# Attention block with routed experts: the positions added by GpSimd before the transposes, the transposed x taken out of PSUM by ScalarE

## The chip, the cores and the metric

The kernel runs on one core of a Trainium2 chip. The metric is the device time of one execution in microseconds (us), the median of several. A core has five engines with instruction streams of their own: TensorE (PE: matmuls and transposes into PSUM), VectorE (DVE), ScalarE (ACT), GpSimd (POOL) and SyncE (SP, which here only issues DMAs). They meet through semaphores. SBUF is the large on-chip memory, PSUM the small one that PE writes.

## The reference

128 sequences of 64 tokens, 128 features each. Cross-attention with 16 heads of 8, then a mixture of 8 experts of which each token takes 2. All of it in float32:

```
n  = layernorm(x)
pe = position encodings, 64 x 128
q  = (n + pe) @ Wq.T + bq          k = (ctx + pe) @ Wk.T + bk        v = ctx @ Wv.T + bv
s  = q.k * 8**-0.5 - 1e7 * (padding mask or causal mask)
x  = x + softmax(s).v @ Wo.T + bo
g  = softmax(gelu(layernorm(x) @ wg1 + bg1) @ wg2), the two largest kept
x  = x + sum over the two experts of g_e * gelu(layernorm(x) @ w_in[e]) @ w_out[e]
```

The change is about the term `n + pe` in the first of these products.

## The kernel before, in words

The 8192 tokens are 64 tiles of 128 rows (two sequences each). A **stage** s is U = 4 tiles; there are NS = 16 stages. The attention part runs the `body(s, i, par)` of each engine for s = 0 to 15, and in each body the four tiles u = 0 to 3. The tile counter is t = 4s + u. No scheduler is at work: every engine's stream is written out by hand, with waits on counters, and what stands where in a body is the order in which it runs.

Per tile, in `body`: PE transposes the probabilities of tile t (L407), makes the scores of tile t+2 into the one score buffer S2 (L391, L397, after `s_sub` says that DVE has emptied it), multiplies with the values (L420, L425) and projects (L434). DVE takes the row maxima of tile t+1 (L814), subtracts them into `sm` (L818), and then divides tile t-1 (L826, L828) and adds the residual of tile t-2 (L836). ACT copies the transposed probabilities out of PSUM (L710) and takes the exponentials of tile t+1 (L652).

Per stage, and one to three stages ahead or behind:

- `ln1_stats` and `ln1_variance` on DVE (L791, L796), `rstd_1` on POOL (L1159 to L1164), `ln1_norm` on ACT (L666), which writes the normalised x, `xn`, of stage s+2 at u = 2.
- `t_x(s+1)` on PE at u = 0 (L362) transposes `xn` into the PSUM bank W0. `x_evac(s+1)` on DVE (L801), still at u = 0, adds the transposed positions `pe_s` and writes `xT`. `project_q(s+1)` on PE at u = 1 (L371) reads it, `q_evac` on ACT (L635) brings q to SBUF.
- `add_positions(s+3)` on POOL at u = 3 (L1150) adds `pe_s` to the context for the keys; `project_k` (L367) and `k_evac` (L631) follow, and SP then spreads the keys to a block layout `kx` with 16 small DMAs (`spread_keys`, L263).
- `make_mask(s+1)` on DVE at u = 0 (L808) reads two SBUF tiles, `mask_in` and `causal`.
- The routing of stage s-2 runs through all engines: ACT `xt2_evac` (L694), `gate_gelu` (L700) and `gate_exp` (L704), PE `gate_hidden` (L464) and `gate_logits` (L470), DVE `take_logits`, `gate_probs`, `find_two_largest` (L876, L878: a small copy from SBUF to SBUF) and `select` (L883, L888). POOL forms the pairs (L1207) and scatters the rows of stage s-3 to HBM with indirect DMAs (L1222). This starts with s = 2; the counting of stage s-3 (L895 to L909 on DVE, the rank matmuls on PE) with s = 3.

Before the first body each engine has a short prologue. ACT issues two lists of constant loads (L657 and L660). The semaphore `s_w` counts the first list, 6 loads, the last of them `bq`; PE, POOL, ACT and DVE wait for all of it. On POOL the prologue is `add_positions(0)`, `rstd_1(0)`, then a memset that clears the second half of `kx` (L1179), then `add_positions(1)`, `rstd_1(1)`. SP waits in L275 for both halves of `kx` to be cleared, and issues `spread_keys(0)` after that; what follows in SP's queue is one long list of issues, up to the keys of stage 2:

```
sp.wait_ge(s_kev, 1)
sp.wait_ge(s_kz, 2)
spread_keys(0)
```

After the attention part the rows are read back in 91 blocks by pair of experts (L583 to L603 on PE, L753 and L770 on ACT, L1103 to L1129 on DVE, L1259 on POOL). The change has nothing in it.

Of the kernel before, what the change touches and what calls it, by code (L numbers as in the profile page):

```python
# [12 lines left out]
ALU = mybir.AluOpType  # L13
# [3 lines left out]
P = 128  # L17
# [56 lines left out]
def build(nc, x, ctxT, mask, wqT, bq, wkT, bk, wvT, bv, woT, bo, wg1, bg1, wg2, w_in, w_out, out):  # L74

    pe_c = nc.inline_tensor(np.ascontiguousarray(position_encodings().T), name="pe_t")
    ident_c = nc.inline_tensor(np.eye(P, dtype=np.float32), name="ident")
# [36 lines left out]
    with ExitStack() as ctx:  # L114
# [35 lines left out]
        xn = sb("xn", [P, U, D])  # L150
        minus_half, eps_s = sb("minus_half", [P, U]), sb("eps_s", [P, U])
# [49 lines left out]
        s_wg2z = sem("wg2_zeroed")  # L201
        s_w2, s_w3 = sem("attention_constants_in"), sem("routing_constants_in")
        NW, NW2, NW3 = 6, 7, 5 + 2 * U
# [39 lines left out]
        with nc.Block() as block:  # L243
# [113 lines left out]
            def _(pe):  # L357
                def t_x(s):

                    pe.wait_ge(s_xn, s + 1)  # L360
                    for u in range(U):
                        last = nc.tensor.transpose(W0[:, u * P:(u + 1) * P], xn[:, u, :], ident[:, :])  # L362
                    last.then_inc(s_xt, 1)
# [264 lines left out]
            def _(act):  # L628
# [8 lines left out]

                def v_evac(s):
                    act.wait_ge(s_v, s + 1)
                    if runs(s, 2):  # L640
                        act.wait_ge(s_pv, (s - 1) * U)
                    src = W0[:, :].rearrange("r (g j p c) -> r g j p c", j=2, p=2, c=DH)
                    for b in range(2):
                        for p in range(2):
                            o = b * VB + p * DH
                            last = nc.scalar.activation(vx[p * 64:p * 64 + 64, s % 2, :, :, o:o + DH],
                                                        src[b * 64:b * 64 + 64, :, :, p, :], ACT.Copy)
                    last.then_inc(s_vev, 1)
# [5 lines left out]
                for dst, src in ((pe_s[:, :], pe_c.ap()), (wk_s[:, :], wkT), (ident[:, :], ident_c.ap()), (wq_s[:, :], wqT),  # L654
                                 (bk_s[:, :], bk.rearrange("(p a) -> p a", a=1)),
                                 (bq_s[:, :], bq.rearrange("(p a) -> p a", a=1))):
                    act.dma_start(dst, src).then_inc(s_w, 16)  # L657
# [22 lines left out]
                k_evac(0, 0)  # L680
                act.wait_ge(s_bqs, 1)
                q_evac(0, 0)
                act.wait_ge(s_xt, 1)
# [22 lines left out]
                def body(s, i, par):  # L706
                    for u in range(U):
# [4 lines left out]
                        if u < U - 1 or runs(s, 0, NS - 2):  # L712
                            exps(t + 1, u + 1)
                        if u == 0 and runs(s, 2):
                            xt2_evac(s - 2)
# [71 lines left out]
            def _(dve):  # L787
# [10 lines left out]

                def x_evac(s):
                    dve.wait_ge(s_xt, s + 1)  # L800
                    nc.vector.tensor_tensor(xT[:, :].rearrange("p (b k) -> p b k", k=L),  # L801
                                            W0[:, :].rearrange("p (b k) -> p b k", k=L),
                                            pe_s[:, :].unsqueeze(1).broadcast_to([P, 2 * U, L]), ALU.add
                                            ).then_inc(s_xTs, 1)
# [181 lines left out]
                x_evac(0)  # L986
# [15 lines left out]
                def body(s, i, par):  # L1002
                    for u in range(U):
# [41 lines left out]
                        if u == 0 and runs(s, 0, NS - 2):  # L1045
                            x_evac(s + 1)
# [98 lines left out]
            def _(pool):  # L1145
# [7 lines left out]

                def rstd_1(s):
# [23 lines left out]
                rstd_1(0)  # L1178
                nc.gpsimd.memset(kx[:, 1, :, :], 0.0).then_inc(s_kz, 1)  # L1179
                pool.wait_ge(s_w2, 16 * NW2)  # L1180
                add_positions(1)
                rstd_1(1)
                pool.wait_ge(s_cvec, 1)
# [42 lines left out]
                def body(s, i, par):  # L1226
                    for u in range(U):
# [16 lines left out]
                        if u == 3 and runs(s, 0, NS - 4):  # L1244
# [4 lines left out]
                            add_positions(s + 3)  # L1249
                        if u == 3 and runs(s, 3, NS - 2):  # L1250
# [58 lines left out]
```

## Time and profile before

| | |
|---|---|
| median of 3 runs | 618.54 us (616.45 to 619.35) |
| the profiled execution, its own time | 617.17 us |
| its span, first to last instruction | 615.4 us |
| DVE busy | 473.8 us, 77% of the span; 96.8% in a stage of the attention part |
| PE busy | 504.6 us, 82% |
| ACT busy | 391.3 us, 64% |
| POOL busy | 272.0 us, 44% |
| attention part | to about 389 us |
| expert part | from there to the end |

In the timelines each line gives the start in us, the busy time in us of the instruction (or of a run of equal ones), engine, line, operation, tiles and shapes, and in brackets the idle time of the engine before it with what ended it. Instructions of one engine are pipelined, so the next can start a little before the one ahead has ended: what an instruction costs its engine is the distance to the next start. SPq, ACTq and POOLq are the DMA-issuing parts of these engines.

### The profile page before, as it was taken

What the parts mean: (1) busy time and instruction counts of PE and PEld (TensorE: products, weight loads), DVE (VectorE), ACT (ScalarE), POOL (GpSimd) and SP (SyncE); (2) the same over time, 40 slices, a digit from 0 to 9 for tenths busy, and PEclk for the clock granted to TensorE, in tenths of its full rate; (3) what the DMA queues carried; (4) which work ended last, traced back from release to release, by engine and by line L of the source; (5) the groups of instructions that cost most, each with busy time, mean ns of one, the idle gap of its engine ahead of it and who ended that gap; (6) DMA issues with size and microseconds to landing.
All of it is one profiled execution on the core that took longest, in us unless ns stands there. A gap on an engine that the chain in (4) does not pass through costs nothing.

```text
span 615.4 us, 19115 instructions
## 1 busy us (share of the span) xinstructions
PE 504.6 (82%) x6643; PEld 383.1 (62%) x6643; DVE 473.8 (77%) x1587; ACT 391.3 (64%) x723; POOL 272.0 (44%) x451
## 2 busy tenths in 40 slices
PE   2489899988988888888998885477577999999992
PEld 0145555645655555554654554377567999999992
DVE  3598899999999999999999997355644666666661
ACT  2156687878878877877787873356333666666660
POOL 4131333463473364365345333345522555555552
PEclk9999999999999999999999997678977999999997
DMA  4137212212212312222111001422555333443300
GB/s 111 17 77 226 62 48 63 75 54 59 79 55 56 84 51 65 71 55 73 32 46 46 20 29 37 125 59 66 170 163 149 103 106 107 108 108 90 80 21 1
DMA packets 41806, 46.86 MB, mean 76 GB/s; under 512 B 9738, under 2 KB 33555, under 8 KB 41248
## 3 DMA queue, kind: packets, MB, share of 16 engines
q1 hardware_dynamic: 34144, 32.28, 20.3%
q0 software_dynamic: 5984, 12.90, 6.2%
q8 instruction: 55, 0.90, 0.6%
q10 hardware_dynamic: 1584, 0.46, 0.3%
q14 instruction: 39, 0.32, 0.2%
HBM read 28.52 MB, written 18.58 MB: 77 GB/s over the span
## 4 chain that ended last, share of the span: by engine, by line
DVE 35%; PE 31%; issue 16%; SPq 12%; DMA 2%; POOL 1%; ACT 1%; ACTq 1%; POOLq 0%; DVEq 0%
PE probs_t L592 13%; PE bank L603 13%; DVE smax L814 10%; DVE rden L826 8%; SPq L263 5%; SPq L322 3%; DVE rows L836 2%; PE scores L583 2%; DVE stat L842 2%; DVE stat L791 1%; DVE negmask L808 1%; DVE left L883 1%; SPq L315 1%; DMA bq_s<-bq 1%; DVE mv L847 1%
## 5 line engine op out<-in xcount | busy, mean ns | idle before, releaser
L1259 POOL DMA_INDIRECT out<-yb,token_row x91 | 89.1, 979 | 108.2 <-DVE token_row L1118 84.7
L592 PE MATMUL probs_t<-xbT,wi 128*128 128x128 f32 x728 | 102.7, 287 | 10.8 <-ACT wi L770 8.3
L753 ACT ACTIVATE hb<-probs_t 128x512 f32<-128x512 f32 x91 | 54.4, 598 | 86.0 <-PE probs_t L592 86.0
L710 ACT ACTIVATE pt<-probs_t 128x1024 f32<-128x1024 f32 x64 | 65.6, 1025 | 66.0 <-PE probs_t L407 65.6
L592 PEld LDWEIGHTS probs_t<-xbT,wi 128*128 128x128 f32 x728 | 94.2, 202 | 12.5 <-ACT wi L770 9.2
L603 PE MATMUL bank<-wo,hb 128*128 x728 | 100.8, 284 | 0.1
L603 PEld LDWEIGHTS bank<-wo,hb 128*128 128x128 f32 x728 | 92.5, 199 | 0.7 <-issue 0.5
L391 PE MATMUL scores<-kx,qT 64*64 64x512 f32 x512 | 70.6, 621 | 27.2 <-DVE sm L818 15.1
L814 DVE TENSOR_REDUCE smax<-scores 128x16 f32<-128x1024 f32 x64 | 77.8, 1216 | 12.1 <-PE scores L397 11.0
L1222 POOL DMA_INDIRECT routed_rows<-rows,pos x64 | 64.2, 1004 | 37.5 <-DVE pos L909 19.5
L818 DVE TENSOR_TENSOR sm<-scores,smax 128x1024 f32<-128x1024 f32 x64 | 78.3, 1224 | 2.2
L1125 DVE SCALAR_TENSOR_TENSOR part<-bank,gate,xb 128x128 f32<-128x128 f32 x91 | 31.9, 350 | 62.0 <-PE bank L603 62.0
L407 PE MATMUL probs_t<-ident_s,sm 128*128 128x128 f32 x512 | 67.7, 276 | 0.9 <-ACT sm L652 0.9
L652 ACT ACTIVATE sm<-sm 128x1024 f32<-128x1024 f32 x64 | 67.3, 1051 | 0.2
L420 PEld LDWEIGHTS bank<-pt,vx 128*32 128x32 f32 x2048 | 31.9, 110 | 54.7 <-DVE onT L828 46.3
L420 PE MATMUL bank<-pt,vx 128*32 128x64 f32 x2048 | 42.3, 223 | 27.5 <-DVE onT L828 26.4
L770 ACT COPY wi<-wi_all 128x256 f32 x182 | 63.7, 402 | 1.2 <-DVE expert_oh L959 1.2
L826 DVE RECIPROCAL rden<-bank 128x128 f32<-128x128 f32 x64 | 60.0, 937 | 2.9 <-PE bank L425 2.9
L407 PEld LDWEIGHTS probs_t<-ident_s,sm 128*128 128x128 f32 x512 | 57.9, 142 | 4.6 <-issue 4.6
L1159 POOL TENSOR_TENSOR var<-mv,eps_s 128x4 f32<-128x4 f32 x16 | 3.2, 201 | 121.4 <-DVE mv L796 116.6
L391 PEld LDWEIGHTS scores<-kx,qT 64*64 64x64 f32 x512 | 13.8, 132 | 59.5 <-DVE sm L818 33.6
L1103 DVE COPY xbT<-scores 128x128 f32<-128x128 f32 x91 | 26.1, 287 | 26.4 <-PE scores L583 26.2
(119 smaller groups left out, 885.9 us busy)
## 6 DMA issues: line engine op xcount, KB each, us to landing
xb<-routed_rows SPq DMA_DIRECT2D x91, 132.5 KB, 2.2
ctx_in<-ctx_t SPq DMA_DIRECT2D x16, 256.0 KB, 3.1
x_in<-x SPq DMA_DIRECT2D x16, 256.0 KB, 3.8
kx<-kT SPq DMA_DIRECT2D x256, 16.0 KB
routed_rows<-padding_rows SPq DMA_DIRECT2D x29, 132.5 KB
out<-yb,token_row POOLq DMA_INDIRECT x91, 2.3
mask_in<-mask SPq DMA_DIRECT2D x16, 64.0 KB, 4.2
wi_all<-w_in SPq DMA_DIRECT2D x1, 1024.0 KB, 9.8
```

Of the source, the lines that this page charges most:

```text
L391: nc.tensor.matmul(S_bank[half][b * L:(b + 1) * L, :].rearrange("p (h k) -> p h k", k=L), qT[r, par, o:o + L], kx[r, par, :, o:o + L], sta ...
L407: last = nc.tensor.transpose(PT_bank[j // 4][:, (j % 4) * P:(j % 4 + 1) * P], pr[:, j * P:(j + 1) * P], ident[:, :])
L420: nc.tensor.matmul(XB[g * VB:(g + 1) * VB, b * L:(b + 1) * L], v[:, c:c + VB], pt[:, 2 * g + j, b * L:(b + 1) * L], start=(j == 0 and b == ...
L592: last = nc.tensor.matmul(UBK[b % 2][:, (2 * j + c) * BLK:(2 * j + c + 1) * BLK], wi[:, b % RH, j, c * P:(c + 1) * P], xbT[:, b % RH, :], ...
L603: last = nc.tensor.matmul(DBK[b % 2][:, j * D:(j + 1) * D], hb[:, b % RH, 2 * j + c, :], wo[:, bass.ds(experts[j], 1), c, :].rearrange("p ...
L652: nc.scalar.activation(sm[:, u % 2, :, :], sm[:, u % 2, :, :], ACT.Exp).then_inc(s_exp, 1)
L710: nc.scalar.activation(pt[:, :, :].rearrange("p j q -> p (j q)"), PT2[:, :], ACT.Copy).then_inc(s_ptev, 1)
L814: nc.vector.reduce_max(smax[:, :], S2[:, :].rearrange("p (h k) -> p h k", k=L), AX).then_inc(s_max, 1)
L818: nc.vector.tensor_tensor(sm[:, u % 2, :, :], S2[:, :].rearrange("p (h k) -> p h k", k=L), smax[:, :].unsqueeze(2).broadcast_to([P, H, L]) ...
L826: nc.vector.reciprocal(rden[:, :], XB[:, P:2 * P]).then_inc(s_rden, 1)
L1222: nc.gpsimd.indirect_dma_start(out=rows_d, out_offset=bass.IndirectOffsetOnAxis(ap=pos[:, r % RR, u:u + 1], axis=0), in_=rows[:, r % RR, u ...
L1259: nc.gpsimd.indirect_dma_start(out=out, out_offset=bass.IndirectOffsetOnAxis(ap=token_row[:, b % RY:b % RY + 1], axis=0), in_=yb[:, b % RY ...
```

## The change

POOL adds the positions, laid out by rows, to `xn` in place (`add_positions_to_x`), ahead of the transposes; PE's `t_x` waits for that instead of for `xn` alone. Since the transposed x then needs nothing added, its way out of PSUM is a plain copy, and it is done by ACT. The row layout of the positions, 128 x 128 floats, is one more constant to load: it stands third in ACT's first list, and `NW` becomes 7. In the prologue POOL's new step stands between `rstd_1(0)` and the memset of `kx`; in the body it stands at u = 3 behind `add_positions(s+3)` and ahead of the fourth scatter. ACT's copy stands at u = 0 behind the exponentials and ahead of `xt2_evac`.

```diff
+    pe_rows_c = nc.inline_tensor(np.ascontiguousarray(np.tile(position_encodings(), (P // L, 1))), name="pe_rows")
...
+        pe_rows = sb("pe_rows_s", [P, D])
...
-        NW, NW2, NW3 = 6, 7, 5 + 2 * U
+        NW, NW2, NW3 = 7, 7, 5 + 2 * U
...
                 def t_x(s):
-                    pe.wait_ge(s_xn, s + 1)
+                    pe.wait_ge(s_xpe, s + 1)
...
+                def x_evac(s):
+                    act.wait_ge(s_xt, s + 1)
+                    nc.scalar.activation(xT[:, :], W0[:, :], ACT.Copy).then_inc(s_xTs, 1)
...
-                for dst, src in ((pe_s[:, :], pe_c.ap()), (wk_s[:, :], wkT), (ident[:, :], ident_c.ap()), (wq_s[:, :], wqT),
+                for dst, src in ((pe_s[:, :], pe_c.ap()), (wk_s[:, :], wkT), (pe_rows[:, :], pe_rows_c.ap()), (ident[:, :], ident_c.ap()), (wq_s[:, :], wqT),
...
                 k_evac(0, 0)
+                x_evac(0)
                 act.wait_ge(s_bqs, 1)
                 q_evac(0, 0)
-                act.wait_ge(s_xt, 1)
                 ln1_norm(1)
...
                             exps(t + 1, u + 1)
+                        if u == 0 and runs(s, 0, NS - 2):
+                            x_evac(s + 1)
                         if u == 0 and runs(s, 2):
                             xt2_evac(s - 2)
...
-                def x_evac(s):
-                    dve.wait_ge(s_xt, s + 1)
-                    nc.vector.tensor_tensor(xT[:, :].rearrange("p (b k) -> p b k", k=L),
-                                            W0[:, :].rearrange("p (b k) -> p b k", k=L),
-                                            pe_s[:, :].unsqueeze(1).broadcast_to([P, 2 * U, L]), ALU.add
-                                            ).then_inc(s_xTs, 1)
...
-                x_evac(0)
+                dve.wait_ge(s_stat, 1)
...
                         if u == 0 and runs(s, 0, NS - 2):
-                            x_evac(s + 1)
                             make_mask(s + 1, 1 - par)
...
+                def add_positions_to_x(s):
+                    pool.wait_ge(s_xn, s + 1)
+                    nc.gpsimd.tensor_tensor(xn[:, :, :], xn[:, :, :], pe_rows[:, :].unsqueeze(1).broadcast_to([P, U, D]),
+                                            ALU.add).then_inc(s_xpe, 1)
...
                 rstd_1(0)
+                add_positions_to_x(0)
                 nc.gpsimd.memset(kx[:, 1, :, :], 0.0).then_inc(s_kz, 1)
...
                 rstd_1(1)
+                add_positions_to_x(1)
                 pool.wait_ge(s_cvec, 1)
...
                             add_positions(s + 3)
+                        if u == 3 and runs(s, 0, NS - 3):
+                            add_positions_to_x(s + 2)
                         if u == 3 and runs(s, 3, NS - 2):
                             scatter_rows(s - 3, (3,))
```

## Rows read from the trace of the kernel before

**Rows 1.** The page: the chain that ended last, shares by engine.
```profile
DVE 35%; PE 31%; issue 16%; SPq 12%; DMA 2%; POOL 1%; ACT 1%; ACTq 1%; POOLq 0%; DVEq 0%
```
**Rows 2.** Busy us of PE, PEld, DVE, ACT, POOL in three stretches: beginning, stages 2 and 8.
```profile
0.00:66.75 66.75, 41.41 (x495) 22.61 (x495) 45.92 (x88) 28.22 (x43) 19.92 (x34) 1.00 0.37 103
66.75:87.99 21.24, 20.90 (x366) 13.08 (x370) 19.32 (x45) 17.66 (x30) 6.03 (x12) 1.00 0.25 66
...
199.34:221.56 22.22, 19.36 (x330) 12.20 (x324) 21.49 (x63) 17.49 (x30) 11.25 (x22) 1.00 0.24 65
```
**Rows 3.** The chain of work to 95 us: start, us, what.
```profile
3.18 5.41 DMA bq_s<-bq
...
11.68 3.45 POOL kx L1179
...
15.21 0.82 SPq L263
...
64.52 1.98 DMA kx<-kT
...
79.16 0.36 PE bank L464 x8
...
85.20 0.88 ACT pt L710
```
**Rows 4.** DVE's timeline of a stage.
```profile
203.53 0.17 DVE L878 COPY two_largest<-largest 128x8 f32<-128x8 f32 x1
...
204.40 0.19 DVE L888 TENSOR_TENSOR chosen<-left,probs 128x32 f32<-128x32 f32 x1
...
208.41 0.68 DVE L801 TENSOR_TENSOR xT<-bank,pe_s 128x512 f32<-128x512 f32 x1
209.01 0.68 DVE L808 SCALAR_TENSOR_TENSOR negmask<-mask_in,causal_s 128x512 f16<-128x512 uint8 x1
```
**Rows 5.** PE's timeline: stage 8's transposes of x, hidden layer, values.
```profile
206.42 0.60 PE L362 MATMUL bank<-ident_s,xn 128*128 128x128 f32 x4
...
210.66 0.43 PE L464 MATMUL bank<-xt,wg_s 128*32 128x128 f32 x8
...
215.59 0.65 PE L420 MATMUL bank<-pt,vx 128*32 128x64 f32 x32 [1.37 <-DVE onT L828]
```
**Rows 6.** ACT's timeline: xt2 of stage 8, and of stage 2.
```profile
209.53 0.59 ACT L694 ACTIVATE xt<-bank 128x512 f32<-128x512 f32 x1
...
78.35 0.59 ACT L694 ACTIVATE xt<-bank 128x512 f32<-128x512 f32 x1
```
**Rows 7.** The first loads: ACT's issues, and size and us to landing.
```profile
1.66 0.53 ACTq L657 DMA_DIRECT2D ident_s<-ident  x1
...
wk_s<-wk_t ACTq DMA_DIRECT2D x1, 64.0 KB, 3.6
ident_s<-ident ACTq DMA_DIRECT2D x1, 64.0 KB, 4.0
```
**Rows 8.** Timelines of the prologue: POOL, ACT and DVE.
```profile
11.61 3.51 POOL L1179 MEMSET kx<- 128x4096 f32 x1
15.08 1.26 POOL L1150 TENSOR_TENSOR ctx_k<-ctx_in,pe_s 128x512 f32<-128x512 f32 x1
...
11.71 1.65 ACT L666 ACTIVATE xn<-x_in,shift,rstd 128x128 f32<-128x128 f32 x4 [3.50 <-POOL shift L1164]
...
15.17 1.72 DVE L808 SCALAR_TENSOR_TENSOR negmask<-mask_in,causal_s 128x512 f16<-128x512 uint8 x1
...
18.00 0.19 DVE L993 COPY bvb_s<-bv_s 128x128 f32<-128x128 f32 x1
```
**Rows 9.** POOL's timeline of a stage: the adds of 128x512.
```profile
201.72 1.29 POOL L1150 TENSOR_TENSOR ctx_k<-ctx_in,pe_s 128x512 f32<-128x512 f32 x1
...
217.84 1.28 POOL L1169 TENSOR_TENSOR x_in<-x_in,cvec 128x512 f32<-128x512 f32 x1
```
**Rows 10.** The groups of instructions: a DVE copy out of PSUM.
```profile
L1103 DVE COPY xbT<-scores 128x128 f32<-128x128 f32 x91 | 26.1, 287 | 26.4 <-PE scores L583 26.2
```

More of the change, by code:

```diff
@@ L201, in build @@
         s_wg2z = sem("wg2_zeroed")
+        s_xpe = sem("positions_added")
         s_w2, s_w3 = sem("attention_constants_in"), sem("routing_constants_in")
-        NW, NW2, NW3 = 6, 7, 5 + 2 * U
+        NW, NW2, NW3 = 7, 7, 5 + 2 * U
         count, blocks_f = sb("count", [P, NP]), sb("blocks_f", [P, 2, NP])
```

## The prediction

> **What bounds the kernel now.** The chain that ended last says which engines to look at: DVE 35%, PE 31%, SP's queue 12% [rows 1]. It covers several regimes, so the next view is the busy time by stage. In a stage such as 8, of 22.2 us, DVE is busy 21.5 us, PE 19.4, ACT 17.5 and POOL 11.3 [rows 2]: DVE is the bound, and its distance from instruction to instruction is what counts. Stage 2 is different: 21.2 us long, DVE busy 19.3 and PE 20.9 [rows 2], because the counting of experts is not yet in it. There, at 79 and 85 us, the chain runs over PE and ACT [rows 3]. Different again is the beginning. From 15.21 us, when SP issues the first key spread, the chain stays in SP's queue up to the last key of stage 2, issued at 64.52 and landed at 66.5; the scores of tile 8 start at 66.75 [rows 3]. SP issues that list back to back (all waits in it are met when it comes to them), so whatever DVE gains before 66.75 is worth nothing, and whatever delays the first spread is paid in full. And the first spread waits for POOL's memset [rows 3]. After about 389 us comes the expert part, in which nothing is changed and which follows the attention part rigidly.
>
> So the change gives in the stages and takes in the prologue, and I cost the two apart.
>
> **What is taken from DVE.** L801 starts at 208.41 and the next instruction at 209.01 [rows 4]: 0.60 us, less than its 0.68 busy because neighbours overlap. There are 15 of them in the bodies, for s = 0 to 14. Those of s = 0 and 1 lie before 66.75 and gain nothing. For s = 3 to 14, 12 stages, the gain must pass PE and ACT to be real. PE stands idle 1.37 us before the values at 215.59, waiting for DVE [rows 5]; that is the first place where PE waits for DVE behind the removed instruction, and 0.60 fits into it. Gain: 12 x 0.60 = **7.2 us**.
>
> **What ACT gets.** One copy of 128x512 out of PSUM, the same form as L694, 0.59 us [rows 6]. It pushes `xt2_evac` back by 0.59. In stage 8 that one ends at 210.12 and PE comes to the hidden layer at 210.66 [rows 5, 6]; moved, it ends at 210.71, and with some 0.07 us of semaphore PE starts at 210.78. PE is 0.12 us late there, ACT 0.2 us at the next copy, and both delays vanish in the 1.37 us before the values. Nothing to pay, as long as that idle time is there. In stage 2 there is no such cover: `xt2_evac` ends at 78.94, the hidden layer starts at 79.16 in the chain [rows 3, 6], directly behind the projection, and PE goes on without a gap. Moved, xt2 ends at 79.53, PE starts at 79.60 instead of 79.09 to 79.16, and the chain passes there, through the next transposes and ACT's copy at 85.20. So stage 2 gains nothing from L801 and loses about **0.5 us** (bounds: 0, and 0.59, the whole copy).
>
> **What PE waits for.** `t_x` now waits for POOL. In stage 8 POOL's add can start when L1150 ends, 203.01, and lasts as long as L1169, which has the same shape and the same broadcast, 1.28 us [rows 9]: it ends at 204.29, and PE comes to the transposes at 206.42 [rows 5]. Covered by 2.1 us. Queued behind it on POOL are one scatter and the pair products, all 1.3 us later; the rank matmuls that need the pairs come some 5 us later still. Nothing.
>
> **What the new add does to DVE.** The stage's timeline does not show it, as nothing of that length reads SBUF on POOL between 203.0 and 204.3 today. But the prologue shows two things. L808, which reads two SBUF tiles, takes 0.68 us [rows 4], and the one that runs beside POOL's add at 15.08 takes 1.72 [rows 8]: it began at 15.17, POOL's add ended at 16.34, and the 1.04 us more are that remainder less 0.13. A two-input DVE instruction stands while POOL reads. And L993, a DVE copy of 128 elements from SBUF to SBUF, takes 0.19 us against 0.29 for L1103, the same shape out of PSUM [rows 8, 10]: it takes two elements at a time, so it too needs a second way into SBUF. In the stage, L878 is such a copy, at 203.53, in the middle of the new add; L888, with two SBUF inputs, is at 204.40, just behind its end [rows 4]. If L878 stands like L808 did, it waits for 204.29 - 203.53 - 0.13 = 0.63 us, and DVE is the bound. Bounds: 0, and the whole remainder of 0.76. I take 0.63, since L808 is the one row that shows such a meeting, at a plain length. It happens where `find_two_largest`, `add_positions` and the new add all stand in u = 3: s = 3 to 12, 10 stages. In s = 2 POOL is free earlier and ends before L878; in s = 13 there is no L1150 ahead, so the new add is over before L878. Cost: 10 x 0.63 = **6.3 us**.
>
> The Trainium skill speaks against the change here. Its page "SBUF — State Buffer", section "Who interferes with whom", says that a DVE instruction with two SBUF inputs contends with a GpSimd instruction that reads SBUF, and that a DVE copy in a two-port mode and a GpSimd instruction block one another fully, whichever starts first; "VectorE: DVE Perf Modes", section "Mode 2×_2P", puts fp32 copies within SBUF with an even outer dimension into that mode. By that rule, the trace agrees for L808, and no row here shows a copy against POOL; by a rule for two-input instructions alone the 6.3 us would be 0.
>
> **The prologue.** First, one more load of 64 KB in the list that `s_w` counts. Its issue costs 0.53 us on ACT's queue, as that of `ident` [rows 7]. The landings are further apart than the issues: `ident` lands at 1.66 + 4.0 = 5.66, `wk`, of the same size, issued 0.53 before it, at 1.13 + 3.6 = 4.73, so 0.93 later. POOL's first add starts when `bq` has landed, 3.18 + 5.41 = 8.59 [rows 3]. I take **0.9 us**, since those two are the same load in the same place; lower bound the bare issue, 0.5, upper 1.3, a little over the widest spacing. Second, POOL's memset (start 11.61) is moved behind `add_positions_to_x(0)`, and that waits for ACT's normalisation: 11.71 + 1.65 = 13.36, plus 0.05 of semaphore, plus 1.28 for the add: 14.69 [rows 8, 9], so **3.1 us** later. SP, waiting for the memset, is late by the sum, 4.0 us; behind that wait stand all 48 key spreads of stages 0 to 2 and the loads between, and so the scores at 66.75. The extra steps of x itself (add, PE, ACT instead of DVE) end near 20 us and the spread keys come only at 31, so they cost nothing.
>
> **The sum.** + 0.9 + 3.1 + 0.5 - 7.2 + 6.3 = **+3.6 us**. Against the profiled execution's own 617.17 us this gives 620.8. That execution lies 1.4 us under the median of 618.54, so for the median I say **622.1**. (A measurement of this kernel can tell about 0.5%, 3.1 us, from no change.)
>
> **The rivals.**
>
> 1. *The small copy does not wait* (faster, or within the 0.5%). L878 has 8 elements, and its rows do not tell one or two at a time. If only two-input instructions wait, L888 starts 0.11 us after the new add ends, and DVE loses nothing. Then the sum is 0.9 + 3.1 + 0.5 - 7.2 = -2.7: 614.5 of its own, 615.8 for the median. What decides is one instruction, L878, under or past 0.2 us. With the cheaper bounds for the load and for stage 2 (0.5 and 0) it is -3.6, 614.9. For it: nothing in the trace of a stage shows a wait of DVE on POOL's reads. Against it: L808 and L993 together. 29%.
> 2. *The prologue is not paid*: SP's list is shortened elsewhere, or POOL's memset is hidden by some wait of SP that the chain does not name. With 6.3 us of stalls the sum is about -0.4 (618.1), without them -6.7 (611.8). Against it: SP's issues follow one another without a gap from 15.21 to 64.52 [rows 3]. 8%, split evenly between the two.
> 3. *ACT becomes the bound* from stage 3 on, as in stage 2: 12 x 0.5 lost in place of the 7.2 gained, which hides the copy's stall behind it. The sum is 4.0 + 0.5 + 6.0 = +10.5: 629.0. Against it: ACT is busy 17.5 of 22.2 us, and 1.37 us of PE's idle lie behind the late point [rows 2, 5]. 5%.
> 4. *No such balance*: POOL's add also holds L888 or other instructions, up to the full 0.76 and more a stage, +5 to +6: near 624. 6%.
>
> That the change does not do what it says can hardly be: the added constant is the same table, and every L801 is gone.
>
> **How the numbers follow.** The forecast has 52%. Its own range, from the bounds of the load (-0.4, +0.4), stage 2 (-0.5, +0.1) and the stall (0.5 to 0.76 us, -1.3 to +1.3), is 620.0 to 623.8. About two thirds of it lie above +3.1 us, one third within 0.5%. Rival 1 lies mostly within 0.5%, about a third of it beyond on the fast side. So: slower 0.34 + rivals 3 and 4 = 0.45; faster 0.10 + half of rival 2 = 0.14; within 0.5% the rest, 0.41. The range has to hold both the forecast and rival 1: 614.8 to 624.0 leaves out about 2 in 10.
>
> **What would show it.** The scores of tile 8 start near 70.7 instead of 66.75 (the prologue, 4.0). POOL's memset starts near 15.6. Stages 3 to 12 stay at about 22.2 us, and 13 and 14 become 0.6 shorter; by rival 1 stages 3 to 14 are all near 21.6. L878 has a few 0.17 us and ten near 0.8. L694 of stage 2 is followed by a hidden layer half a microsecond late. ACT is busy 9 us more, POOL 20 more, DVE's L801 (10.9 us) is gone. If the scores of tile 8 move by less than 3 us, or L878 stays at 0.17, the forecast is wrong.

## The result and the profile after

| | before | after |
|---|---|---|
| median | 619.27 us (13 runs, 616.45 to 624.45) | 622.63 us (13 runs, 620.26 to 626.93) |
| profiled execution: own time, span | 617.17, 615.4 us | 623.51, 621.6 us |
| ratio of the times, with its 95% interval | | 1.0058 [1.0029, 1.0086] |

The change makes the kernel slower by 3.4 us (0.58% by the ratio of the runs), where 3.6 us had been forecast (622.1 for the median). The interval lies wholly above 1. The profiled execution of after lies 0.9 us above its median, that of before 2.1 under its own, so what follows adds up to 6.2 us of span and not to 3.4. The page of after, busy times and the shares of the chain that ended last; ACT has 8 us more, POOL 20 more, DVE 5 less, and the chain is as it was [rows 1]:

```profile
PE 510.0 (82%) x6643; PEld 385.7 (62%) x6643; DVE 468.6 (75%) x1571; ACT 399.1 (64%) x739; POOL 292.4 (47%) x467
...
DVE 34%; PE 30%; issue 16%; SPq 12%; ACT 2%; DMA 2%; POOL 1%; ACTq 1%; POOLq 0%; DVEq 0%
```

To see where the time went, both traces are laid beside each other at fixed marks. The mark of a stage is the start of the first `smax` behind its `probs`, which bounded the windows of before too [rows 2]; behind the `probs` of mark 14 there is no `smax`, so this mark is the start of the next `rden`.

| place | before | after | later by |
|---|---|---|---|
| first key spread issued by SP | 15.21 | 18.80 | 3.59 |
| scores of tile 8 start | 66.75 | 70.22 | 3.47 |
| their `smax` starts | 68.16 | 72.74 | 4.58 |
| mark 1, end of stage 2 | 87.99 | 93.03 | 5.04 |
| mark 2 | 110.20 | 114.65 | 4.45 |
| mark 12 | 332.70 | 337.12 | 4.42 |
| mark 13 | 353.88 | 357.70 | 3.82 |
| mark 14 | 378.74 | 382.62 | 3.88 |
| first block of the expert part | 392.45 | 397.00 | 4.55 |
| last block | 600.06 | 606.32 | 6.26 |

So the prologue and stage 2 take 5.0 us, the twelve windows from mark 1 to mark 13 give 1.2 back, and the rest of the 6.2 arises in the expert part. That part has no edit in it; from mark 14 to the last block it took 221.3 us before and 223.7 after, and between 221.9 and 223.3 in the profiles of the four variants of the first group below, which share one chip; it follows neither the adds nor the copy. I put that down to scatter and not to the change.

**The prologue.** POOL of after, its timeline. The memset of `kx` started at 11.61 before [rows 8] and starts at 15.20 now. The first add starts only 0.08 later than before (8.72). Between the two stand the add to x, with its wait for ACT, and one thing that was not foreseen: `shift<-mv,minus_one` takes 0.67 us, where the same instruction takes 0.20 ten microseconds later.

```profile
8.80 1.26 POOL L1151 TENSOR_TENSOR ctx_k<-ctx_in,pe_s 128x512 f32<-128x512 f32 x1 [7.89 <-DMA bq_s<-bq]
...
10.17 0.67 POOL L1166 TENSOR_TENSOR shift<-mv,minus_one 128x4 f32<-128x4 f32 x1
...
14.00 1.26 POOL L1157 TENSOR_TENSOR xn<-xn,pe_rows_s 128x512 f32<-128x512 f32 x1 [1.76 <-ACT xn L673]
15.20 3.51 POOL L1186 MEMSET kx<- 128x4096 f32 x1
...
20.04 0.20 POOL L1166 TENSOR_TENSOR shift<-mv,minus_one 128x4 f32<-128x4 f32 x1
```

DVE's timeline at that place shows what stood against it: with `x_evac(0)` gone DVE comes to `make_mask(0)` at 10.08, not at 15.17 [rows 8], and this instruction with two SBUF inputs is under way when POOL comes to its own at 10.17.

```profile
10.08 0.69 DVE L810 SCALAR_TENSOR_TENSOR negmask<-mask_in,causal_s 128x512 f16<-128x512 uint8 x1 [1.24 <-DMA wo_s<-wo_t]
```

The chain of waits of after, where it can be set beside that of before [rows 3]: the same stations. `bq` is issued 0.48 us later but has landed only 0.07 later (8.66 against 8.59); from the memset on all is later by 3.5 us or so, and behind tile 8 by 5.

```profile
3.66 5.00 DMA bq_s<-bq
...
15.20 3.52 POOL kx L1186
...
18.80 0.82 SPq L266
...
67.99 1.99 DMA kx<-kT
...
70.22 1.98 PE scores L394 x8
...
84.13 0.43 PE bank L467 x8
```

**The clock at tile 8.** The last station but one holds the second thing that was not foreseen: eight matmuls take 1.98 us, where before they took 1.09. The busy time by stretch shows PE's granted clock there, third number from the right, first after, then before (columns as in rows 2): 0.66 and 1.00, that is, part of the stretch at 1.2 GHz against all of it at 2.4. PE had stood idle 2.08 us ahead of those scores, waiting for the keys, against 1.75 before.

```profile
70.00:75.00 5.00, 4.78 (x68) 2.78 (x69) 2.23 (x2) 1.39 (x4) 2.67 (x3) 0.66 0.49 130
```

```profile
70.00:75.00 5.00, 4.66 (x80) 3.21 (x79) 4.85 (x7) 3.78 (x7) 0.00 (x0) 1.00 0.14 27
```

**The stages.** The windows of after by stage; the second is that of the same stage as 199.34 to 221.56 before [rows 2]. The first is 0.6 shorter than its 22.21 of before, the second as long as it was.

```profile
93.03:114.65 21.62, 19.26 (x326) 12.12 (x321) 20.90 (x62) 18.41 (x32) 9.65 (x20) 1.00 0.19 48
...
203.39:225.60 22.21, 19.75 (x330) 12.36 (x323) 21.35 (x62) 17.98 (x31) 12.48 (x23) 1.00 0.24 65
```

What makes the difference stands in DVE's timeline (the one at 118.83) and in the group of L880, the former L878: minimum, median and maximum of 16 are 171, 628 and 756 ns. The copy beside the new add takes 0.75 us, `chosen` behind it is not touched. In time the sixteen are 0.17, then ten of 0.42 to 0.76, then five of 0.17 to 0.18.

```profile
118.83 0.75 DVE L880 COPY two_largest<-largest 128x8 f32<-128x8 f32 x1
...
120.28 0.19 DVE L890 TENSOR_TENSOR chosen<-left,probs 128x32 f32<-128x32 f32 x1
...
L880 DVE COPY two_largest<-largest x16: 171/628/756, 97.2 to 428.7; 128x8 f32<-128x8 f32 x16
```

```profile
117.04 1.28 POOL L1151 TENSOR_TENSOR ctx_k<-ctx_in,pe_s 128x512 f32<-128x512 f32 x1
118.27 1.27 POOL L1157 TENSOR_TENSOR xn<-xn,pe_rows_s 128x512 f32<-128x512 f32 x1
```

POOL's timeline (the second fence) has the new add from 118.27 to 119.54; the copy ends at 119.58.

### The profile page after: what moved, and what is told of

It is laid out like the page before. It is cut to its first block, busy times and chain, and to the rows that moved or that the text cites. A ratio compares the mean times of both kernels' runs of the same rounds, so it can differ in the third digit from the quotient of the medians.

```text
span 621.6 us, 19131 instructions
## 1 busy us (share of the span) xinstructions
PE 510.0 (82%) x6643; PEld 385.7 (62%) x6643; DVE 468.6 (75%) x1571; ACT 399.1 (64%) x739; POOL 292.4 (47%) x467
## 4 chain that ended last, share of the span: by engine, by line
DVE 34%; PE 30%; issue 16%; SPq 12%; ACT 2%; DMA 2%; POOL 1%; ACTq 1%; POOLq 0%; DVEq 0%
PE probs_t L595 13%; PE bank L606 13%; DVE smax L816 10%; DVE rden L828 8%; SPq L266 5%; SPq L325 3%; DVE rows L838 2%; DVE stat L844 2%; PE scores L586 2%; DVE stat L800 2%; DVE left L885 1%; DVE two_largest L880 1%; SPq L318 1%; DMA xb<-routed_rows 1%; DMA bq_s<-bq 1%
## 5 line engine op out<-in xcount | busy, mean ns | idle before, releaser
L394 PE MATMUL scores<-kx,qT 64*64 64x512 f32 x512 | 72.4, 636 | 31.4 <-DVE sm L820 18.2
```

The costliest lines, as they stand in the source:

```text
L394: nc.tensor.matmul(S_bank[half][b * L:(b + 1) * L, :].rearrange("p (h k) -> p h k", k=L), qT[r, par, o:o + L], kx[r, par, :, o:o + L], sta ...
```

## The experiments

Twelve kernels ran, in three groups, each group on a chip of its own with the kernel before beside it. On the first chip before took 618.79 us (31 runs), much as in the comparison above; on the second 639.10 (16 runs), on the third 636.10 (23 runs). Times are therefore compared within a group only.

### First group: one part at a time

**e1_memset_first**, the memset of `kx` back ahead of the new step.

```diff
-                add_positions_to_x(0)
                 nc.gpsimd.memset(kx[:, 1, :, :], 0.0).then_inc(s_kz, 1)
+                add_positions_to_x(0)
```

> The changed kernel with one swap in POOL's prologue: the memset of kx stands ahead of the first add of positions to x again, as in the kernel before. Theory (the memset's place is the largest term of the prologue, 3.0 us, and with it the 1.1 us that TensorE lost at 1.2 GHz in the scores of tile 8): the first key spread starts near 15.8 us, not 18.8, the scores of tile 8 near 67.2, not 70.2, and the time is 3 to 4 us under the changed kernel's, about 619, equal to the kernel before. Rival (the spread waits for something else that came late too, such as the keys or the load): the first spread stays past 18 us and the time near 622.6.

Measured: 618.22 us, 0.9996 [0.9964, 1.0029] of before, so the loss is gone. The memset starts at 11.98, the first spread at 15.58, the scores of tile 8 at 66.82, within 0.1 us of before, and they take 1.09 us again. Mark 1 is at 88.43 (before 87.99): stage 2 is still 0.4 us longer. The copies of the stages still take up to 0.745 us. POOL's timeline:

```profile
11.98 3.51 POOL L1185 MEMSET kx<- 128x4096 f32 x1
15.45 1.26 POOL L1157 TENSOR_TENSOR xn<-xn,pe_rows_s 128x512 f32<-128x512 f32 x1
```

One line of order carries nearly the whole loss of the prologue: 3.2 us at the first spread (18.80 to 15.58), 3.4 by the scores of tile 8 and 1.1 of clock, 4.5 in sum.

**e2_copy_as_reduce**, the small copy written as a maximum over an axis of length 1, the same values.

```diff
-                    nc.vector.tensor_copy(two_largest[:, :, 0:KTOP], largest[:, :, 0:KTOP]).then_inc(s_ch, 1)
+                    nc.vector.reduce_max(two_largest[:, :, 0:KTOP], largest[:, :, 0:KTOP].unsqueeze(3), AX).then_inc(s_ch, 1)
```

> The changed kernel, with the small copy in find_two_largest written as a maximum over an axis of length one: the same elements from SBUF to SBUF, but an operation with one input that is not a copy. Theory (the copy stands because it takes its elements over both of DVE's ways into SBUF, and a reduction does not): the instruction takes about 0.17 us in all 16 stages, not 0.75, and the time is 5 to 6 us lower, near 617. Rival (any DVE instruction that comes at this point beside POOL's add stands, whatever its kind): the reduction takes 0.6 to 0.8 us in ten stages, and the time stays near 622.6.

Measured: 616.34 us, 0.9955 [0.9929, 0.9981], though the prologue is as late as after (scores of tile 8 at 70.25 and 1.87 us long). The groups of this kernel: the reduction takes 0.16 us each of the 16 times, `chosen` at most 0.23.

```profile
L880 DVE TENSOR_REDUCE two_largest<-largest x16: 161/162/163, 97.3 to 425.0; 128x8 f32<-128x8 f32 x16
...
L890 DVE TENSOR_TENSOR chosen<-left,probs x16: 191/200/227, 98.1 to 425.8; 128x32 f32<-128x32 f32 x16
```

From mark 1 to mark 13 it takes 259.8 us against 264.7 after and 265.9 before. The stall of one 8-element copy is worth 4.9 us, and without it the change gives 6.1 in the stages.

**e3_no_add**: POOL's adds are left out altogether, so the positions are missing from the queries; PE waits for `xn` as before, the copy on ACT stays.

```diff
-                    pe.wait_ge(s_xpe, s + 1)
+                    pe.wait_ge(s_xn, s + 1)
...
-                add_positions_to_x(0)
...
-                add_positions_to_x(1)
...
-                        if u == 3 and runs(s, 0, NS - 3):
-                            add_positions_to_x(s + 2)
```

> The changed kernel with POOL's adds to x left out altogether (the positions are missing from q; the load, ScalarE's copy and the missing DVE step are as in the changed kernel). It shows what taking the step from DVE is worth by itself. Theory: the prologue is late by 0.1 to 0.6 us, stage 2 by 0.5, and 12 stages are 0.60 shorter: 6 to 6.7 us under the kernel before, near 612.5. Rival (ScalarE's copy costs in all stages, or the gain is lost in the waits between the engines): less than 3 us under the kernel before.

Measured: 614.24 us, 0.9940 [0.9908, 0.9972], 4.6 us under before, where 6 to 6.7 had been expected. First spread 15.13, scores of tile 8 at 66.58. Mark 1 is at 88.20: stage 2 takes 21.62 us here too, so its 0.4 to 0.5 is due to ACT's copy and not to the adds. Mark 1 to 13 takes 260.0 us, the same as e2 within 0.2. The two ways of removing the stall, from DVE's side and from POOL's, agree. The gain is 5.9 us instead of the forecast 7.2: nine of the twelve windows are 0.48 to 0.65 shorter, but three only 0.15 to 0.34. What holds DVE in those three isn't resolved. Two copies, in the third and the sixth window, take 0.27 and 0.38 us although there is no add; the second of them, and POOL's timeline beside it:

```profile
201.20 0.38 DVE L880 COPY two_largest<-largest 128x8 f32<-128x8 f32 x1
```

```profile
200.62 0.98 POOL L1228 DMA_INDIRECT routed_rows<-rows,pos  x1 [0.17 <-issue]
```

Both begin late in the fourth scatter (0.58 us into it here, 0.69 in the other) and end as it ends; the eight copies that begin 0.34 to 0.36 into it take 0.17.

**e4_before_idle_add**: the kernel before, with an add on POOL of the same size at the same place, whose result nobody uses.

```diff
+                            if runs(s, 1):
+                                act.wait_ge(s_idle_add, s)
                             ln1_norm(s + 2)
...
+                        if u == 3 and runs(s, 0, NS - 3):
+                            pool.wait_ge(s_xn, s + 3)
+                            if s:
+                                pool.wait_ge(s_idle_add, s)
+                            nc.gpsimd.tensor_tensor(spare[:, :, :], xn[:, :, :], cvec[:, :].unsqueeze(1).broadcast_to([P, U, D]),
+                                                    ALU.add).then_inc(s_idle_add, 1)
```

> The kernel before, with one more add on POOL in the bodies, of the same shape and at the same place as the changed kernel's, whose result nobody reads; nothing else is touched. Theory (the stall of DVE's small copy is a cost of its own, apart from everything else in the change): the copy takes about 0.75 us in ten stages and the time is 5 to 6 us above the kernel before, near 624.5. Rival (the stall only filled time that the removed step had left free): the time is within 2 us of the kernel before.

Measured: 623.50 us, 1.0088 [1.0063, 1.0114]. The group of the copy:

```profile
L882 DVE COPY two_largest<-largest x16: 172/740/752, 91.7 to 430.4; 128x8 f32<-128x8 f32 x16
```

The typical stage takes 22.80 us instead of 22.22. From mark 1 to 13 it is 5.8 us longer than before, ten times 0.58. So the cost comes with the add alone, with PE and the prologue as they were. ACT only gets a wait for that add before it writes `xn` again, and its list of waits in this trace has none for it.

### Second group: better places, and what kind of work on POOL stops the copy

**e5_adds_apart**: the memset first; the context add moved to u = 0 behind `pair_of`, so that POOL comes to the add to x earlier in u = 3; and `xt2_evac` ahead of the copy on ACT.

```diff
-                        if u == 0 and runs(s, 0, NS - 2):
-                            x_evac(s + 1)
                         if u == 0 and runs(s, 2):
                             xt2_evac(s - 2)
+                        if u == 0 and runs(s, 0, NS - 2):
+                            x_evac(s + 1)
...
-                add_positions_to_x(0)
                 nc.gpsimd.memset(kx[:, 1, :, :], 0.0).then_inc(s_kz, 1)
+                add_positions_to_x(0)
...
+                        if u == 0 and runs(s, 1, NS - 3):
+                            add_positions(s + 2)
...
-                        if u == 3 and runs(s, 0, NS - 4):
-                            if runs(s, 2):
-                                pool.wait_ge(s_ch, (s - 2) * CH + 4)
-                            else:
-                                pool.wait_ge(s_norm, s * U + 2)
-                            add_positions(s + 3)
```

> The change, with four steps put elsewhere: the memset of kx first in the prologue; in the bodies the add to x alone at u = 3, ahead of the fourth scatter, the add to the context behind the pair products of the next body (u = 0, stage s+2 there), and xt2_evac ahead of x_evac on ScalarE. Theory (the change's own worth is 0.60 us in each of 12 stages, and what eats it is where the adds meet DVE): the small copy takes 0.17 us in all stages, stage 2 is as long as before, and the time is 6 to 7 us under the kernel before, a ratio near 0.989. Rival (an add of 1.28 us on POOL meets some DVE instruction wherever it stands, or the context's add comes late for TensorE): ratio 0.995 or more, with another DVE instruction or TensorE seen waiting.

Measured: 635.08 us, 0.9918 [0.9887, 0.9948], faster than before on that chip by 0.8%. That is 4.0 us, less than the 6 to 7 expected, and stage 2 is not as short as before but takes 22.8 us: PE's granted clock is at 0.50 from 68.6 to 72.0, right behind the scores of tile 8. No copy stands any more:

```profile
L880 DVE COPY two_largest<-largest x16: 172/173/182, 94.2 to 435.4; 128x8 f32<-128x8 f32 x16
```

**e6_xt2_first**: e1 with the two copies on ACT exchanged, the first hunk of e5.

> The changed kernel with the memset of kx first (as in e1) and xt2_evac ahead of x_evac on ScalarE. Theory (stage 2 loses time because ScalarE's new copy pushes xt2_evac back, and TensorE waits for that): from the scores of tile 8 to the first maxima of tile 12 it is about 21.2 us, as in the kernel before, and not 21.6 as in e1; the gate's hidden layer does not wait for ScalarE. Rival (the copy delays ScalarE's later work, whatever stands first): 21.6 us again.

Measured: one run, 630.82 us. This is the miss that corrects a step of the prediction. PE no longer waits for `xt`: its hidden layer starts at 79.01. Yet stage 2 takes 21.61 us, from 66.67 to 88.28, as without the exchange (21.61 in e1). PE and then ACT:

```profile
79.01 0.43 PE L467 MATMUL bank<-xt,wg_s 128*32 128x128 f32 x8
...
84.37 1.09 PE L410 MATMUL probs_t<-ident_s,sm 128*128 128x128 f32 x8
```

```profile
83.26 1.06 ACT L659 ACTIVATE sm<-sm 128x1024 f32<-128x1024 f32 x1
```

The transposes at 84.37 come when the exponentials of 83.26 are done. ACT has no idle time from its copy of the probabilities at 76.41 up to them; both copies and two loads of its function table, 1.28 us each, stand in that stretch, so the order of the copies doesn't matter. In the kernel before, the same exponentials start at 82.91 and PE comes to the transposes at 84.13 without waiting. The late hidden layer was not the path. (Before takes 21.24 us for stage 2 in both of its traces, `before` and e12, so the comparison over chips holds.)

**e7_add_after_scatter**: e1 with the add to x moved behind the fourth scatter.

```diff
-                        if u == 3 and runs(s, 0, NS - 3):
-                            add_positions_to_x(s + 2)
                         if u == 3 and runs(s, 3, NS - 2):
                             scatter_rows(s - 3, (3,))
+                        if u == 3 and runs(s, 0, NS - 3):
+                            add_positions_to_x(s + 2)
```

> The changed kernel with the memset of kx first (as in e1), and in the bodies the add to x one step later on POOL, behind the fourth scatter. Theory (DVE instructions with two inputs in SBUF stand as well while POOL reads): the small copy, which now meets the end of the context's add at most, takes 0.17 us again, and the comparison behind it, which has two inputs in SBUF, takes 1 us or more instead of 0.19 in ten stages; stages are longer than 22.2 us. Rival (only copies stand): the comparison takes 0.19 us and the stages are near 21.6.

Measured: one run, 646.04 us, the slowest of its group, and not as expected: `chosen` stays at 0.19 and the copy itself is worse, up to 2.0 us. DVE first, the group and one of them; then POOL's timeline beside it.

```profile
L880 DVE COPY two_largest<-largest x16: 172/871/2007, 94.5 to 446.9; 128x8 f32<-128x8 f32 x16
...
116.13 2.00 DVE L880 COPY two_largest<-largest 128x8 f32<-128x8 f32 x1
```

```profile
115.78 0.99 POOL L1230 DMA_INDIRECT routed_rows<-rows,pos  x1 [0.17 <-issue]
116.80 1.29 POOL L1157 TENSOR_TENSOR xn<-xn,pe_rows_s 128x512 f32<-128x512 f32 x1
```

The copy stands from 116.13, 0.67 us before the add starts, and ends with the add. It begins 0.35 us into the scatter. In the kernel before the copies begin 0.34 to 0.41 into the same scatter, and all take 0.17. So at this place the scatter alone doesn't hold them (later in it, it can: the two copies of e3); with the add queued behind it the copy stands through both. Two copies are of this kind (2.00 and 2.01 us); the nine others that are held begin inside the add.

**e8_before_idle_memset**: the kernel before with a memset on POOL in the place of e4's add, about as long, which writes SBUF and reads nothing.

```diff
+                            nc.gpsimd.memset(spare[:, :], 0.0).then_inc(s_idle_add, 1)
```

> The kernel before with a memset of about 1.3 us on POOL at the place of the changed kernel's add: it writes SBUF and reads nothing. Theory A (the copy needs the way by which POOL writes, too): the small copy takes 0.7 us or more in ten stages, as with the add in e4. Theory B (only POOL's reading stops DVE): it takes 0.17 us in all, and the time is that of the kernel before.

Measured: one run, 641.48 us. The group of the copy on DVE; then one copy, and POOL's timeline beside it.

```profile
L880 DVE COPY two_largest<-largest x16: 172/173/205, 94.5 to 443.9; 128x8 f32<-128x8 f32 x16
...
302.38 0.19 DVE L880 COPY two_largest<-largest 128x8 f32<-128x8 f32 x1
```

```profile
301.23 1.31 POOL L1256 MEMSET spare<- 128x1440 f32 x1
```

All copies are short, but this does not speak for theory B, because they do not meet the memset. In nine of the ten stages the copy starts 0.08 to 0.20 us after the memset has ended, since DVE comes to it 1.15 us or more behind the start of POOL's instruction here, and 0.6 us behind it in e4. The one shown is the only one that meets it, with 0.16 us of it left: a stall by the rule of the others, the remainder less 0.13, would give 0.20, which can't be told from 0.19.

A meeting that does decide stands in the prologue of the kernels that clear `kx` first. DVE's copy `bvb_s<-bv_s`, also from SBUF to SBUF, takes 0.19 us where no memset runs on POOL [rows 8]. In e6 it comes 0.47 us into the memset, DVE first and then POOL:

```profile
12.34 3.12 DVE L995 COPY bvb_s<-bv_s 128x128 f32<-128x128 f32 x1
```

```profile
11.87 3.51 POOL L1185 MEMSET kx<- 128x4096 f32 x1
```

It is done 0.08 us after the memset. So it is in all eight traces of kernels in which the memset runs at this time (e1, e3, e5, e6, e7, e9, e10 and e11; 2.99 us in e3, 3.12 in the others), and in none of the other six. So work on POOL that only writes holds a copy too, as theory A has it. It cost nothing here: DVE's next instruction, a memset that doesn't wait for the copy, starts 1.20 us behind the copy's start, in e6 as in after. Whether an instruction with two SBUF inputs is held by a POOL instruction that only writes, no run shows.

The Trainium skill, "SBUF — State Buffer", section "Who interferes with whom", calls the pair of ports shared by the two engines one exclusive lock: a DVE instruction in a two-port mode and a GpSimd instruction block each other fully, while a reduction never contends on this chip. By that rule, e2 and e4 agree (0.16 and 0.74 us), and so does the copy beside the memset (3.12 us).

### Third group: are there versions that beat both, and whose are the odd waits

**e9_memset_first_reduce**: e1 and e2 together.

> The two repairs of e1 and e2 together and nothing else: the memset of kx first in the prologue, and the small copy written as a reduction. Theory (the two are independent, one in the prologue and one in the stages): 622.6 less about 4 and about 6 us, 612 to 613, a ratio to the kernel before of 0.988 to 0.991. Rival (part of the two gains is the same gain): a ratio of 0.994 or more.

Measured: 632.53 us (12 runs), 0.9940 [0.9912, 0.9967], where 0.988 to 0.991 had been expected. Both repairs work: the memset starts at 11.94, and all reductions take 0.16 us. But the scores of tile 8 follow 2.57 us of idle PE and take 1.24 us, the clock falls during them, and stage 2 takes 22.8 us; the stages lose time in waits that e12 takes up. The stretch 70 to 75, columns as in rows 2:

```profile
70.00:75.00 5.00, 5.00 (x62) 3.40 (x55) 4.05 (x6) 1.97 (x2) 0.00 (x0) 0.83 0.15 29
```

**e10_adds_apart_again**: e5 once more, unchanged.

> The kernel of e5 again, beside the kernel before and e9 in the same job. In e5 stage 2 and several later stages held waits of 0.7 us and more that no kernel had shown before, on signals from TensorE. Theory (those belong to that chip and that execution, not to the order of the adds): here every stage from 3 on takes about 21.6 us, stage 2 about 21.6, and the ratio to the kernel before is 0.988 to 0.991, as for e9. Rival (the new order makes them): they are here again, but not in e9.

Measured: 632.92 us (12 runs), 0.9951 [0.9928, 0.9973]. The copy is at 0.17 to 0.18 again and stage 2 takes 21.6 us. The rest of the expectation missed (a ratio of 0.988 to 0.991, all stages near 21.6): the first window takes 21.6 us, the next ten 22.0 to 22.8.

**e11_reduce_add_after_scatter**: e7 with the reduction of e2.

> The kernel of e7 with the small copy written as a reduction. In e7 the copy stood for the add, and so the comparison behind it never met the add. Theory (a DVE instruction with two inputs in SBUF stands as well): the reduction takes 0.17 us, and the comparison, with both inputs in SBUF, takes 0.8 us or more in place of 0.19 in ten stages. Rival (only copies stand): the comparison stays at 0.19 to 0.25 us.

Measured: one run, 633.15 us. With the copy out of the way DVE reaches `chosen`, which has two SBUF inputs, while the add runs, and now that one stands. It is 0.97 to 1.15 us in four stages and 0.25 to 0.33 in five, in which it catches only the end of the add (expected were 0.8 or more in ten); each time it is done 0.06 us or so after the add:

```profile
L890 DVE TENSOR_TENSOR chosen<-left,probs x16: 191/264/1148, 93.3 to 437.1; 128x32 f32<-128x32 f32 x16
...
115.12 0.97 DVE L890 TENSOR_TENSOR chosen<-left,probs 128x32 f32<-128x32 f32 x1
```

```profile
114.74 1.29 POOL L1157 TENSOR_TENSOR xn<-xn,pe_rows_s 128x512 f32<-128x512 f32 x1
```

**e12_before_again**: the kernel before, unchanged, for its trace on this chip.

> The kernel before, unchanged, for its trace on the chip of this job. Theory: stages of 22.2 us as in the first trace, if the chip is like the first; if the kernel before takes near 639 us here, its stages hold the same waits of 0.7 us and more on TensorE's signals as e5 did, which then belong to the chip. Rival: stages of 22.2 us and the extra time elsewhere.

Measured: 635.14 us. DVE's and ACT's timelines have waits whose releaser the trace only calls remote, and that the first chip's profiles of before and after don't have:

```profile
135.89 0.96 DVE L826 RECIPROCAL rden<-bank 128x128 f32<-128x128 f32 x1 [0.68 <-remote]
...
135.96 1.02 ACT L710 ACTIVATE pt<-probs_t 128x1024 f32<-128x1024 f32 x1 [2.63 <-remote]
```

In the case shown PE's last matmuls before, the transposes that ACT waits for, had ended at 134.41. Since the unchanged kernel has these waits, they belong to the chip (or to that hour), not to any edit. But they don't strike all kernels alike. The view of waits gives sum, count and longest for DVE, in e12, e10 and e9 in this order:

```profile
DVE rden L826 <- remote: 2.9, 4, 0.8
```

```profile
DVE rden L828 <- remote: 6.7, 9, 0.9
```

```profile
DVE rden L828 <- remote: 5.6, 8, 0.8
```

On that chip a part of what DVE gains is waited away again: from mark 1 to mark 13 before takes 270.5 us, e9 266.3, so 4.2 us gained, where e2 against before gained 6.1 on the first chip. What the remote waits are is open.

## Why the prediction was right

**Result and size.** Forecast +3.6 us against measured +3.4: slower by over 0.5%, the likeliest of the three, though the interval [1.0029, 1.0086] reaches into the band called no change. It came out right with three terms of the prologue off, by -0.8, +0.5 and +1.1 us, which partly cancel, and a stall a little cheaper than forecast. That it came within 0.2 us is luck; the large terms, of the memset, of L801 and of the copies, are not.

- **The extra load, +0.9: too large.** It was sized by the spacing of two landings. The wait for `bq` ended 0.08 us later, about 0.1. It was under the lower bound of 0.5 too: the issue of `bq` did come 0.48 later, but its transfer then took 5.00 us in place of 5.41, so the landing is not set by the issue alone. Over all traces POOL's first add starts at 8.51 to 9.03 us without the extra load and at 8.56 to 9.10 with it, so its cost does not stand out of the scatter.
- **A meeting on POOL, +0.5: not in the sum.** `shift<-mv,minus_one` was held by DVE's `negmask` from 10.17. The prediction had looked at the meeting L808 with POOL's add [rows 8] as DVE's loss only, and had not asked where `negmask` goes once `x_evac(0)` ahead of it is gone. The other traces bear it out. Whichever POOL instruction begins while `negmask` runs is long: `rstd` with 1.37 to 1.57 us in place of 1.04 (e1, e2, e5, e6, e9, e10), `var` with 0.71 in place of 0.19 (e7, e11). In e3, where `rstd` begins 0.03 us before `negmask`, and in the four traces with `negmask` near 15 us, none is.
- **The memset behind the new add, +3.1: right.** From POOL's first add to the memset it was 2.89 us before and is 6.40 now; of the 3.51 more, some 0.5 is the meeting, so 3.0 the step. e1, by undoing this order, takes the spread back to 15.58.
- **SP's list pays it in full: right.** 3.59 us at its first issue arrive as 3.47 at the scores of tile 8. The forecast had 4.0 at both.
- **PE's clock at tile 8, +1.1: not in the sum.** The delay grows from 3.47 to 4.58 in one group of eight matmuls. The prediction priced the wait for the keys, not what the wait does to the instructions behind it.
- **Stage 2, +0.5: size right, path wrong.** It is 0.46 after, 0.37 in e1. The prediction had it pass through the hidden layer that waits for `xt2_evac`. e6 took that wait away and gained nothing there: the path is ACT's own queue, on which one more 0.59 us copy stands ahead of the exponentials. The forecast had looked at ACT's copy and at the wait right behind it, not at what ACT has to do until the next wait of PE. That the size fits is luck.
- **L801 off DVE, -7.2 in 12 stages: right by the window.** The first and the last of the twelve windows, in which no copy stands, are 0.59 and 0.60 shorter. e2 and e3 show 6.1 and 5.9 in place of 7.2 for all twelve: three or four of them gain less, for a cause left open.
- **The small copy, +6.3 in 10 stages: right.** Ten copies, in the stages named. 0.58 us extra where it stands in full (0.75 less 0.17) against 0.63; 0.25 and 0.34 in two of them, 5.3 in sum. By the difference of after and e2 it is 4.9 us; by e4, where all ten stand nearly in full, 5.8. Rival 1, that the copy doesn't wait, had the time of 615.8; e2 makes that rival real, with its 616.3.
- **The stages in sum**: -0.9 forecast, -1.2 measured.

With the marks: 0.1 + 0.5 + 3.0, less 0.1 won inside SP's list, + 1.1 + 0.5 is 5.1 against 5.04 at mark 1; less 1.2 is 3.8 at mark 13, and the forecast had 3.6. The other two microseconds of the profiled execution are the expert part's scatter, and they are not in the medians. Rivals 2 (prologue hidden), 3 (ACT becomes the bound) and 4 (more is held) fall in the kernel as changed: tile 8 was late, the ACT-bound stage stayed the one it was, and `chosen` stayed at 0.19. The mechanism of rival 4 exists, though, as e7 and e11 show; it needs the add one scatter, 1.0 us, later.

**What is better than both.** e5, measured twice on two chips, is faster than before by 0.8% and by 0.5%, e9 by 0.6%, and e2 on the first chip by 0.45%; all four intervals lie under 1. The idea of the change, taking the add from the busiest engine, is sound. It was worth about 6 us in the stages; its two placements, of the memset behind a waiting add in the prologue and of the add beside a copy in the stages, cost 4.5 and about 5. e5 and e9 weren't run on the first chip.

## What to carry to other kernels

Before work is moved to GpSimd, look at what VectorE does in that microsecond. Even an 8-element copy from SBUF to SBUF stands until GpSimd's instruction ends, and so does anything with two SBUF inputs beside a GpSimd instruction that reads. The price is the remainder of the GpSimd instruction, not the size of the copy. It falls on VectorE's own time where the next instruction waits for the copy, as in the stages here; in e6's prologue the next one didn't wait for it and was not late. Write such a copy as a reduction, or move the GpSimd work to where VectorE reads PSUM (the division at 201.74 in the kernel before takes 0.95 us beside POOL's add of 201.72, and 0.95 at 74.52 with POOL idle). And in a prologue, put the instruction that releases a long DMA list ahead of anything that waits for another engine.

## What was not expected of the hardware

- Holding goes both ways: POOL's 128x4 instruction took 0.67 us in place of 0.20 when a VectorE instruction with two SBUF inputs had begun 0.09 us before it, and in eight other traces one of its neighbours was longer by 0.3 to 0.5 us in the same way.
- With an add queued on POOL behind an indirect DMA's issue the copy stands before the add has begun: 2.00 us in e7, begun 0.67 us before the add, where the same DMA without an add behind it leaves a copy that begins at the same place in it at 0.17. Two copies that begin later in it, 0.58 and 0.69 us, are held to its end (e3: 0.38 and 0.27).
- Work on POOL that only writes holds a copy too: 3.12 us in place of 0.19 beside the memset of `kx` in e6, done 0.08 us after it, while DVE's next instruction starts as if the copy were not late.
- What TensorE's clock does behind a wait isn't told by the wait's length alone: it was kept after 2.12 us idle (e3), and fell after 2.04 (e7), 2.08 (after), 2.11 (e2), 2.15 (e5), 2.57 (e9) and 2.76 (e8). Where it fell within the next eight matmuls they took 1.24 to 1.98 us instead of 1.09; in e5 it fell right behind them. What decides it is open.
- The unchanged kernel took 618.8, 639.1 and 636.1 us on three chips, 3% apart, with waits on two of them that the trace can't name.
